# A 64-expert layer's sorted half: all eight places of a token by one best-8 call on coded ranks

## The reference

```
h = silu(y @ w_gate[e]) * (y @ w_up[e])
out += share[token, e] * (h @ w_down[e])      for the token's eight experts e
```

## Time and profile before

| what | value |
|---|---|
| three runs | 1983.6, 1998.93, 2015.92 us |
| the profiled execution, its own time | 1998.39 us |
| its span, first to last instruction | 1996.6 us |
| TensorE busy | 1734.6 us, 87% of the span |
| VectorE busy | 1160.7 us, 58% |
| ScalarE busy | 961.8 us, 48% |
| GpSimd busy | 701.4 us, 35% |
| mean granted TensorE clock | 0.922 of full speed |

### The profile page before, as it was taken

How to read it: one execution, slowest core, us unless ns; L and a number is a source line. 1 busy time by engine, 2 the same in 40 slices (tenths; PEclk the granted TensorE clock), 3 DMA queues, 4 the chain that set the end, 5 groups by cost and what they waited for, 6 DMA issues and landing times. The chain is left out here.

```text
span 1996.6 us, 50161 instructions
## 1 busy us (share of the span) xinstructions
PE 1734.6 (87%) x19970; PEld 1209.3 (61%) x19970; DVE 1160.7 (58%) x2432; ACT 961.8 (48%) x2303; POOL 701.4 (35%) x944
## 2 busy tenths in 40 slices
PE   7883898784699999999999788889997999999885
PEld 4332898443457888888887644557984556633332
DVE  4534334439666777777874335756656766934434
ACT  4551433457676666666664353224542241066552
POOL 1004120304356767676765101462036310044201
PEclk9997898896789999999999897999999996999998
DMA  7302576200031000000000040424632100000100
GB/s 283 167 2 80 164 214 182 58 0 0 1 127 56 24 14 24 14 24 14 24 14 25 13 190 16 124 74 124 170 111 68 47 1 1 1 1 1 39 1 23
DMA packets 75641, 125.69 MB, mean 63 GB/s; under 512 B 10696, under 2 KB 55120, under 8 KB 73776
## 3 DMA queue, kind: packets, MB, share of 16 engines
q1 hardware_dynamic: 67408, 106.69, 16.8%
q0 software_dynamic: 6912, 15.61, 2.5%
q10 hardware_dynamic: 1088, 0.13, 0.0%
HBM read 83.73 MB, written 38.67 MB: 61 GB/s over the span
## 5 line engine op out<-in xcount | busy, mean ns | idle before, releaser
L2884 DVE SCALAR_TENSOR_TENSOR big<-bank,pack,big 128x256 f32<-128x256 f32 (+2 forms) x384 | 182.8, 477 | 41.8 <-ACT mask L2773 24.7
L2772 ACT ACTIVATE big<-bank,pack 128x256 f32<-128x256 f32 x192 | 90.8, 473 | 129.6 <-PE bank L2580 125.3
L2107 ACT ACTIVATE pack<-bank 128x512 f32<-128x512 f32 x96 | 57.5, 600 | 190.7 <-PE bank L785 101.5
L783 PE MATMUL bank<-yh,wl 128*128 128x512 f32 x192 | 114.6, 597 | 29.6 <-DVE a L2262 17.8
L2490 POOL TENSOR_TENSOR big<-big,mask 128x256 f32<-128x256 f32 (+1 forms) x128 | 93.9, 734 | 91.2 <-DVE big L2884 59.1
L2567 PE MATMUL bank<-big 128*128 128x128 f32 x896 | 124.0, 286 | 1.8 <-issue 1.7
L2580 PE MATMUL bank<-y,pack 128*128 128x262 f32 (+1 forms) x384 | 120.9, 400 | 4.9 <-DVE big L2884 4.7
L3284 ACT ACTIVATE pt<-bank 128x1024 f32<-128x1024 f32 (+3 forms) x128 | 79.6, 706 | 91.5 <-PE bank L3136 91.5
L1906 POOL DMA_INDIRECT pack<-results,where x64 | 64.5, 1007 | 154.9 <-DMA results<-a 116.4
L3066 POOL TENSOR_SCALAR_AFFINE_SELECT pt<-pt 128x256 f32<-128x256 f32 x128 | 55.1, 442 | 175.1 <-ACT pt L3284 172.8
L1150 DVE SCALAR_TENSOR_TENSOR a<-bank,big,a 128x128 f32<-128x128 f32 x184 | 51.8, 343 | 106.1 <-ACT a L1062 68.5
(11 more groups left out here) (663 smaller groups left out, 4525.4 us busy)
## 6 DMA issues: line engine op xcount, KB each, us to landing
big<-in_experts SPq DMA_DIRECT2D x46, 516.0 KB
big<-in_big SPq DMA_DIRECT2D x1, 9216.0 KB, 26.2
gate<-big SPq DMA_DIRECT2D x32, 256.0 KB
z<-gate SPq DMA_DIRECT2D x16, 512.0 KB, 3.5
pack<-routing SPq DMA_DIRECT2D x60, 128.0 KB
wide_sorted<-big SPq DMA_DIRECT2D x5, 1472.0 KB, 13.0
pack<-in_pack SPq DMA_DIRECT2D x1, 5910.5 KB, 21.5
pack<-wide_sorted SPq DMA_DIRECT2D x16, 256.0 KB, 3.2
```

Source lines behind the costliest of these rows:

```text
L783: nc.tensor.matmul(out, pl, dh[:, cur], start=start, stop=False)
L2772: nc.scalar.activation(dst3(i), conv_in(i, 0), ACT.Copy, scale=weight(i, 3))
L2884: ins = nc.vector.scalar_tensor_tensor(out=d, in0=conv_in(i, back), scalar=weight(i, 3 - back), in1=d, op0=ALU.mult, op1=ALU.add)
```

## The change

The rank and the place of a kept expert become one number, `rank * 128 * 128 + at`, over all 64 experts of a token (`code`). `at` is below 128 * 128, so one `max` call for each tile of tokens returns the eight numbers of the kept experts, the highest rank first. A constant `codes` (128 x 8), made by GpSimd early in the layer, is subtracted to leave the places, and one cast writes all 64 columns of `where`, now with the eight places of a tile of tokens side by side. `placed` is raised once. The scatter's two loops change places and lose the waits between. `share` is selected as before, with the ranks counted down (`weigh`). `place` moves from unit 7 to unit 6, `locate` and `situate` from block 4 to block 3, all of `put` stands behind block 4. WIDE_SPLIT becomes 26, and WIDE_MIX_AT, which is computed from it, moves by two units.

```diff
--- before.py
+++ after.py
@@ -24,7 +24,7 @@
 BIG0_AT = 14336
 EXPERT_GROUPS = ((0, 1), (2, 3))
 WIDE_TILES = (2 * S * 8 + 64 * (P - 1)) // P
-WIDE_SPLIT, WIDE_POOLED, WIDE_PLACE_AT, WIDE_MAP_AT = 25, 6, 7, 13
+WIDE_SPLIT, WIDE_POOLED, WIDE_PLACE_AT, WIDE_MAP_AT = 26, 6, 6, 13
 WIDE_MIX_AT = [2 * WIDE_SPLIT + 8 + 9 * i // 2 for i in range(8)]
 SORTED = (max(len(g) for g in EXPERT_GROUPS) * 2 * S + 8 * (P - 1)) // P
 
@@ -1798,7 +1798,7 @@
         top, mx, every = sb("top", HALF * 8), sb("mx", HALF), sb("every", HALF)
         where, share, spot = sb("where", K8 * HALF, I32), sb("share", K8 * HALF), sb("spot", K8 * HALF)
         need, upto, base = sb("need", G), sb("upto", G), sb("base", G)
-        whole, number, expert, first_col = sb("whole", K8 + 1, I32), sb("number", K8 + 1), sb("expert", 1), sb("first_col", 2 * P, I32)
+        whole, number, codes, expert, first_col = sb("whole", K8 + 1, I32), sb("number", K8 + 1), sb("codes", K8), sb("expert", 1), sb("first_col", 2 * P, I32)
         own = [k.dead[:, (2 * i) * S:(2 * i + 2) * S] for i in range(2)]
         sc, sel = [m[:, 0:S] for m in own], [m[:, S:2 * S] for m in own]
         tmp = sc[0]
@@ -1885,6 +1885,8 @@
             nc.gpsimd.iota(whole[:, K8:], pattern=[[1, 1]], base=0, channel_multiplier=1).then_inc(s["counted"], 1)
             pool.wait_ge(s["counted"], 2)
             nc.gpsimd.tensor_copy(number[:, :], whole[:, :]).then_inc(s["numbered"], 1)
+            pool.wait_ge(s["numbered"], 1)
+            nc.gpsimd.tensor_scalar(codes[:, :], number[:, 0:K8], -float(P), float(K8 * P * P), ALU.mult, ALU.add).then_inc(s["numbered"], 1)
             nc.gpsimd.memset(restart, 1.0).then_inc(s["counted"], 1)
             pool.wait_ge(s["counted"], 3)
             nc.gpsimd.memset(tile(restart)[:, :, 0:1], 0.0).then_inc(s["numbered"], 1)
@@ -1894,16 +1896,16 @@
                 split(m)
             pool.wait_ge(k.wide_cleared, 16 * -(-WIDE_TILES // SORTED))
             pool.wait_ge(s["rows_ready"], 2)
-            for c in range(K8):
-                pool.wait_ge(s["placed"], c + 1)
-                for i in range(HALF):
-                    nc.gpsimd.indirect_dma_start(out=rows_in, out_offset=bass.IndirectOffsetOnAxis(where[:, c * HALF + i:][:, 0:1], 0), in_=y[:, sl(i, P)], in_offset=None).then_inc(s["scattered"], 16)
+            pool.wait_ge(s["placed"], 1)
+            for i in range(HALF):
+                for c in range(K8):
+                    nc.gpsimd.indirect_dma_start(out=rows_in, out_offset=bass.IndirectOffsetOnAxis(where[:, i * K8 + c:][:, 0:1], 0), in_=y[:, sl(i, P)], in_offset=None).then_inc(s["scattered"], 16)
             for slot in range(4):
                 pool.wait_ge(s[f"stored_{slot}"], 16 * len(range(slot, PAIRS, 4)))
             for i in range(HALF):
                 after(pool, s["mixed"], i - 1)
                 for c in range(K8):
-                    nc.gpsimd.indirect_dma_start(out=found[:, sl(i % 2 * K8 + c, P)], out_offset=None, in_=rows_out, in_offset=bass.IndirectOffsetOnAxis(where[:, c * HALF + i:][:, 0:1], 0)).then_inc(s[f"got_{i % 2}"], 16)
+                    nc.gpsimd.indirect_dma_start(out=found[:, sl(i % 2 * K8 + c, P)], out_offset=None, in_=rows_out, in_offset=bass.IndirectOffsetOnAxis(where[:, i * K8 + c:][:, 0:1], 0)).then_inc(s[f"got_{i % 2}"], 16)
 
         @block.tensor
         def _(pe):
@@ -1944,7 +1946,7 @@
             def place():
                 pe.wait_ge(s["odd"], 3)
                 pe.wait_ge(s["even"], 3)
-                pe.wait_ge(s["numbered"], 4)
+                pe.wait_ge(s["numbered"], 5)
                 pe.wait_ge(s["picked_bf"], 1)
                 pe.wait_ge(s["rows_ready"], 2)
                 nc.tensor.matmul(spots, later_bf[:, :], picked_bf[:, :], start=True, stop=False)
@@ -2209,7 +2211,7 @@
                 dve.wait_ge(s["picked"], 1)
 
             def order():
-                dve.wait_ge(s["numbered"], 2)
+                dve.wait_ge(s["numbered"], 3)
                 link(nc.vector.tensor_tensor_scan(rank, restart, sel[1], 0.0, ALU.mult, ALU.add))
 
             def order_kept():
@@ -2228,13 +2230,20 @@
                 tiled = base[:, :].unsqueeze(1).broadcast_to([P, HALF, G])
                 link(nc.vector.scalar_tensor_tensor(out=tile(at), in0=tiled, scalar=float(P), in1=tile(spots), op0=ALU.mult, op1=ALU.add))
 
-            def pick(dst, c, values):
-                link(nc.vector.scalar_tensor_tensor(out=tmp, in0=rank, scalar=float(c + 1), in1=values, op0=ALU.is_equal, op1=ALU.mult))
-                link(nc.vector.tensor_reduce(dst[:, sl(c, HALF)], tile(tmp), AX.X, ALU.add))
-
-            def put(c):
-                pick(spot, c, at)
-                nc.vector.tensor_copy(where[:, sl(c, HALF)], spot[:, sl(c, HALF)]).then_inc(s["placed"], 1)
+            def weigh(c):
+                link(nc.vector.scalar_tensor_tensor(out=tmp, in0=rank, scalar=float(K8 - c), in1=sc[1], op0=ALU.is_equal, op1=ALU.mult))
+                link(nc.vector.tensor_reduce(share[:, sl(c, HALF)], tile(tmp), AX.X, ALU.add))
+
+            def code():
+                link(nc.vector.scalar_tensor_tensor(out=tmp, in0=rank, scalar=float(P * P), in1=at, op0=ALU.mult, op1=ALU.add))
+
+            def put():
+                for t in range(HALF):
+                    ins = nc.vector.max(spot[:, sl(t, K8)], tmp[:, sl(t, G)])
+                link(ins)
+                coded = spot[:, :].rearrange("p (i c) -> p i c", c=K8)
+                link(nc.vector.tensor_tensor(coded, coded, codes[:, :].unsqueeze(1).broadcast_to([P, HALF, K8]), ALU.subtract))
+                nc.vector.tensor_copy(where[:, :], spot[:, :]).then_inc(s["placed"], 1)
 
             def map_tiles():
                 link(nc.vector.tensor_scalar(need[:, :], upto[:, :], number[:, K8:], None, ALU.is_le))
@@ -2331,11 +2340,12 @@
                 if m == 2:
                     order()
                     order_kept()
-                if m == 4:
+                if m == 3:
                     locate()
                     situate()
-                if m >= 4 and m % 2 == 0 and m // 2 - 2 < K8:
-                    put(m // 2 - 2)
+                if m == 4:
+                    code()
+                    put()
                 if m == 5:
                     map_tiles()
                 if m == 7:
@@ -2350,7 +2360,7 @@
                 if p == 6:
                     link(nc.vector.tensor_tensor(tile(sc[1]), tile(sc[1]), wide(mx), ALU.mult))
                 if p >= 8 and p % 4 == 0 and p // 4 - 2 < K8:
-                    pick(share, p // 4 - 2, sc[1])
+                    weigh(p // 4 - 2)
                 if p > 1:
                     evict(p - 2)
             for m in range(WIDE_SPLIT, J):
```

## The result

The changed kernel takes 2039.24 us (median of four executions, 2036.57 to 2041.26); beside it the kernel before takes 1994.24 us. The ratio is 1.0243, 95% interval 1.0191 to 1.0295: slower by some 45 us. Forecast were 2003 us, with a range from 1982 to 2024. The profiled execution takes 2041.26 us, 42.9 us more than the one of before.

A forecast was written before the change was run, and what follows sets the result against it. TensorE, busy 89% of both dense stretches, was taken as the bound, with its signals late beside unbroken GpSimd issuing. 1998.4 - 1.0 - 0.3 + 6.2 + 0 gave 2003 us, range 1982 to 2024.

The forecast's parts named there:

- Selections: VectorE ahead of the tiles: eight selections of 12.6 us become 2.3 us in block 4; 1.0 us gained (0 to 4.7).
- places: Places computed earlier, blocks 3 and 4: TensorE's wait at unit 12 shrinks from 1.28 to about 1.0 us; 0.3 gained.
- counts: One more small GpSimd operation early in the layer and two raised semaphore counts, reached long before block 2: 0.
- the earlier end of the scatter: Scatter's last issue ends near 1348 us instead of 1360.4; nobody gains by it: 0.
- the 26th block: One block of 4.5 us moves ahead of the tiles: 0, or up to 4.5 us lost if the gather paces.
- What the pauses gave: Unbroken scatter row ahead of the tiles: 15 us free, then 3.3 us a unit for 71 us; 6.2 us lost.
- Behind the tiles: Dense stretch after the tiles: about 122 us expected, with the moved block gone from it.
- A: Rival: lateness follows the number of issues, not their spacing; only VectorE's saving counts, 1997 us, chance 0.25.
- B: Rival: lateness comes once in a row and dies out while GpSimd still issues; 1985 us, chance 0.17.
- C: Rival: late rate as in the stretches before the tiles, 3.9 us a unit; 2011 us, chance 0.18 with worse.

The follow-up runs named there:

- g1: Kernel before, with GpSimd writing an unread tile four times behind every four scatter issues; 2006.43 us, 1.0061 of the kernel before.
- f3: Changed kernel, with GpSimd writing an unread tile four times behind every four scatter issues; 1992.34 us, 0.9997 of the kernel before.
- e3: Changed kernel with 25 blocks ahead of the tiles and 7 behind, as before the change; 2039.24 us, 1.0172 of the kernel before.
- f4: Changed kernel with every second scatter issue left out, 32 issues without a pause; 1997.10 us, one execution.
- e4: Changed kernel with the old order of the 64 scatter issues, still without a pause; 2027.04 us, 1.0112 of the kernel before.
- f1: Changed kernel, with GpSimd writing an unread tile seven times behind every eight scatter issues; 1990.90 us, 0.9984 of the kernel before.
- e2: Kernel before, with its eight selections in one piece at block 4, so the scatter runs unbroken; 2031.26 us, 1.0143 of the kernel before.
- g4: Changed kernel, with GpSimd writing an unread tile once behind every two scatter issues; 1984.87 us, 0.9955 of the kernel before.
- g3: Changed kernel with two GpSimd writes behind every four scatter issues, 27 blocks ahead of the tiles, token sums every fourth unit; 1978.22 us, 0.9966 of the kernel before.
- g2: Changed kernel, with GpSimd writing an unread tile twice behind every four scatter issues; 1984.23 us, 0.9974 of the kernel before.

## Why the prediction was wrong

*Selections, places, counts, the earlier end of the scatter, the 26th block: right within their bounds.* The selections are worth 0 where no unit is late (g1 against f3); their 1.0 us was forecast for the late stretches, where no run shows them alone. TensorE's wait at unit 12 fell from 1.28 us to 0.28, 1.0 gained and not 0.3 (bounds 0 and 1.3):

```profile
1258.79 0.49 PE L783 MATMUL bank<-yh,wl 128*128 128x512 f32 x1 [0.28 <-DVE a L2271]
```

The product (0.68), best-8 (1.12), subtraction (0.22) and cast (0.20) are 2.2 us, forecast 2.3. The row of issues is 81.5 us long, forecast 84. The 26th block costs 1.9 us of the layer by e3's trace, forecast 0 (up to 4.5).

*What the pauses gave: the step that failed.* Its mechanism was right: the pauses were what kept the signals from being late, and the row without them is late until it ends. Its size was not: +6.2 us were forecast, at most +30, and ahead of the tiles 45.3 us were lost. The free time was 8 us, not 15, and the rate was not 3.3 us a unit, the mean of all five late stretches, but grew from 5 to 21.7 us a unit. The five stretches were each ended by a pause after 12 to 29 us; they are beginnings of a lateness that f4 shows growing with the length of the row. A mean over beginnings was carried to a row of 84 us, and the worst of them, 6.7 us a unit, was taken for the end of the term, though nothing showed that the rate stops there. The range was closed at 2024 us, below even the 2027 us that this end gives (1998.4 - 1.3 + 30), and a time slower by 2% had a chance of 0.03 on the ground that it needed more than this rate; the second half of the row ran at three times that.

*Behind the tiles: put at nothing, and not so in this execution.* 122 us were forecast and 134.0 measured. Silu's group there, in the kernel before and in the changed one:

```profile
L2107 ACT ACTIVATE pack<-bank 128x512 f32<-128x512 f32 x46 | 27.6, 600 | 91.3 <-PE bank L785 50.1 <-remote 22.7 <-DVE a L2262 12.6
...
L2109 ACT ACTIVATE pack<-bank 128x512 f32<-128x512 f32 x44 | 26.3, 600 | 99.5 <-PE bank L785 46.6 <-remote 32.4 <-DVE a L2271 10.6
```

Some 10 us more stand on "remote". Whether the change brings this is open: e4, with the same gather, has 22.5 us there. In the profiled execution these 12 us are balanced by the 12.8 us that the other layers took less; that the whole, 42.9 us, comes so near to the 45.3 lost ahead of the tiles is luck.

*The rivals.* A (lateness follows the number of issues) falls with f1 and f3: all 64 issues, no lateness. B (it dies out) falls with the silus at 1322 and 1344. C named the right side and the right place, with the same error in its rate; its reason against itself, that a steady late row would not repeat the slower clock, failed too (0.50 to 0.58 from 1281.6 to 1344.1). The Trainium skill's rule that TensorE never waits on anyone ("SBUF — State Buffer", section "SBUF: two separate sides") speaks of ports, and nothing here shows a port; taken as "GpSimd can't hold TensorE up" it doesn't hold, with silu's 72.7 us on "remote" ahead of the tiles and none in f1 and f3.

*What stays open.* Why the signal is late. By the order of the matmuls above the delay lies between a product's end and the start of what waits for it; no view shows where. The Trainium skill ("Perfetto Trace Analysis", section "Tensor Engine Instruction (MATMUL, LD_WEIGHTS)") places the acknowledgement of the written bytes and the spreading of the signal behind the end that the profile models. The order of the matmuls agrees with a delay there; no run shows which of the two it is. Nor is it settled why the layers behind differ by up to 18 us between executions, why a row goes free for 8 to 9 us in the changed kernel and its unpaused variants, for 10 to 22 us in the kernel before and for 26 us in e2, or how much the gather's lateness varies by itself (21.6 to 32.4 us on "remote" with the same gather in f1, g4 and the changed kernel).

## What to carry to other kernels

A wait that an edit takes away may be what keeps two engines out of each other's way: where a loss begins some time into a busy row and ends with a pause, ask what it would be in a longer row, and don't carry the mean of short ones over. Where GpSimd issues many indirect DMAs beside a TensorE pipeline of short steps, other GpSimd work of 0.6 us behind every two issues made 64 issues 23 us longer here and took 68 us of lateness away. Independent work moved in front of the transfer's end may buy back what such pauses cost: with 27 blocks in place of 26 the layer was 2.1 us shorter in g3 than in g2, which the times don't tell apart.

## What the runs showed that was not expected

Of the engines in this chain TensorE's signals come late beside indirect DMA issues at 1.27 us each: after some 8 us in the changed kernel, growing to one unit (a gate and an up signal) in 21.7 us, about 17 issues. Those of ScalarE and VectorE reach TensorE at once there: its next matmul starts 0.74 us after a late silu's start (1300.66 to 1301.40) and after that of a VectorE product (1288.73 to 1289.47), which last 0.60 and 0.69 us. The 0.30 us between issues doesn't help; 0.6 us of other work behind two issues does (late 1 us), GpSimd being busy all the time. Half the rows in an issue change nothing (71 us late, 22 us a unit). And while TensorE stands its clock falls: the granted clock of the late stretches is 0.50 to 0.58, and 1.00 in the same place with pauses (f3). What that costs beside the late signals was not measured.
